# Cross attention: value and output weights multiplied per head, probabilities packed, and the load of projected values issued ahead of the store

## What is computed

```python
h1 = adaln(x, t, norm1_w, norm1_b)
x = mha(h1, h1, attn1_wq, attn1_wk, attn1_wv, attn1_wo, attn1_bo) + x
h2 = adaln(x, t, norm2_w, norm2_b)
x = mha(h2, context, attn2_wq, attn2_wk, attn2_wv, attn2_wo, attn2_bo) + x
...
    scores = jnp.einsum('bhqd,bhkd->bhqk', q, k) / math.sqrt(DH)
    attn = jax.nn.softmax(scores, axis=-1)
    out = jnp.einsum('bhqk,bhkd->bhqd', attn, v)
    out = out.transpose(0, 2, 1, 3).reshape(b, sq, INNER)
    return out @ wo + bo
```

## Time and profile before

| | before |
|---|---|
| median of 3 runs | 931.8 us (930.72 to 932.12) |
| the profiled execution | 932.87 us, span 931.1 us |
| mean granted clock of TensorE | 0.917 |
| busy: PE, PEld | 796.0 us (85%), 666.3 us (72%) |
| busy: DVE, ACT, POOL | 568.6 (61%), 540.7 (58%), 360.9 us (39%) |
| L685, transposes of probabilities | 512 records, 77.7 us |
| L697, probabilities by values | 1024 records, 70.2 us |
| L650 on oTB, output product | 256 records, 32.9 us |
| L641 on ctxT, value projection | 36 records in the trace, 18.6 us |

### The profile page before, as it was taken

How to read it: one execution, slowest core, us unless ns; L and a number is a source line. 1 busy time by engine, 2 the same in 40 slices (tenths; PEclk the granted TensorE clock), 3 DMA queues, 4 the chain that set the end, 5 groups by cost and what they waited for, 6 DMA issues and landing times.

```text
span 931.1 us, 19002 instructions
## 1 busy us (share of the span) xinstructions
PE 796.0 (85%) x6173; PEld 666.3 (72%) x6173; DVE 568.6 (61%) x1941; ACT 540.7 (58%) x1147; POOL 360.9 (39%) x559
## 2 busy tenths in 40 slices
PE   5989999999999999999987688999977776861693
PEld 4767778878788888888866456999746565651693
DVE  1687778777776767766674352333458787885012
ACT  3656677666776667666764222333448898851462
POOL 1344344333433323233655150566413222226362
PEclk9999999999999999999998689999956979795797
DMA  9532033206030001000200131888500000001574
GB/s 280 198 129 107 1 129 129 106 2 231 5 120 34 19 2 37 16 23 16 65 12 19 46 105 47 241 252 246 201 18 1 1 0 1 1 1 38 164 204 125
DMA packets 43612, 78.50 MB, mean 84 GB/s; under 512 B 5564, under 2 KB 28812, under 8 KB 42876
## 3 DMA queue, kind: packets, MB, share of 16 engines
q1 hardware_dynamic: 40027, 70.09, 23.5%
q0 software_dynamic: 3488, 7.20, 2.2%
HBM read 63.98 MB, written 30.13 MB: 101 GB/s over the span
## 4 chain that ended last, share of the span: by engine, by line
PE 56%; DVE 21%; issue 8%; ACT 6%; POOL 6%; DMA 2%; DVEq 0%; SPq 0%; ACTq 0%; POOLq 0%
PE bank L635 6%; PE bank L909 5%; PE bank L697 5%; PE bank L660 4%; PE bank L650 3%; DVE sb_smax L1406 3%; PE bank L641 3%; PE bank L685 3%; PE bank L669 3%; PE bank L917 3%; DVE sb_row_sum L1416 3%; PE bank L1018 2%; DVE sb_st_all L1714 2%; PE bank L726 2%; PE bank L1026 2%
## 5 line engine op out<-in xcount | busy, mean ns | idle before, releaser
L1891 POOL TENSOR_TENSOR sb_expd<-sb_expd,sb_rden 128x512 f32<-128x512 f32 (+1 forms) x128 | 112.5, 880 | 248.3 <-DVE sb_rden L1420 248.2
L1406 DVE TENSOR_REDUCE sb_smax<-bank 128x4 f32<-128x512 f32 (+1 forms) x128 | 74.1, 579 | 59.1 <-PE bank L660 34.8
L1983 POOL TENSOR_TENSOR sb_rstd_all<-sb_rsq_all,sb_halves 128x4 f32<-128x4 f32 x44 | 45.2, 1028 | 130.7 <-DVE sb_rsq_all L1721 130.7
L685 PE MATMUL bank<-sb_eye,sb_expd 128*128 128x128 f32 (+1 forms) x512 | 77.7, 279 | 5.8 <-POOL sb_expd L1891 5.3
L1128 ACT ACTIVATE sb_expd<-sb_shifted 128x512 f32<-128x512 f32 (+1 forms) x128 | 69.8, 545 | 19.0 <-DVE sb_shifted L1409 18.0
L685 PEld LDWEIGHTS bank<-sb_eye,sb_expd 128*128 128x128 f32 (+1 forms) x512 | 60.0, 145 | 26.4 <-issue 13.2
L1122 ACT ACTIVATE sb_probT<-bank 128x512 f32<-128x512 f32 (+1 forms) x128 | 74.3, 590 | 7.2 <-PE bank L685 7.0
L1409 DVE TENSOR_TENSOR sb_shifted<-bank,sb_smax 128x512 f32<-128x512 f32 (+1 forms) x128 | 75.0, 586 | 4.4
L1416 DVE TENSOR_REDUCE sb_row_sum<-sb_expd 128x4 f32<-128x512 f32 (+1 forms) x128 | 73.0, 570 | 5.5 <-ACT sb_expd L1128 5.5
L635 PE MATMUL bank<-sb_h1T,sb_watt 128*128 128x128 f32 x512 | 71.6, 286 | 4.7 <-ACT sb_h1T L1045 2.3
L697 PE MATMUL bank<-sb_probT,sb_v 128*64 128x128 f32 (+1 forms) x1024 | 70.2, 279 | 5.0 <-issue 3.4
(11 more groups left out here) (256 smaller groups left out, 1905.7 us busy)
## 6 DMA issues: line engine op xcount, KB each, us to landing
sb_up_w<-gate_up SPq DMA_DIRECT2D x38, 384.0 KB, 4.1
rows_b<-pad_b SPq DMA_DIRECT2D x7, 1105.0 KB, 8.5
rows_a<-pad_a SPq DMA_DIRECT2D x7, 975.0 KB, 6.4
sb_up_w<-w1b SPq DMA_DIRECT2D x23, 256.0 KB, 3.5
sb_v<-v_all SPq DMA_DIRECT2D x16, 308.0 KB
v_all<-sb_v_rows SPq DMA_DIRECT2D x9, 512.0 KB, 2.6
sb_blk_x<-rows_a SPq DMA_DIRECT2D x38, 65.0 KB, 3.0
sb_watt<-att_w SPq DMA_DIRECT2D x4, 512.0 KB, 6.6
```

What stands on the lines that cost most here:

```text
L685: mm = pe.transpose(trans[u % 2][0:n, h, :], expd[:, (units_before(i) + u) % EXP_RING, h, 0:n], eye[:, :])
L1406: dve.tensor_reduce(smax[:, u % 2, :], s_in, X, ALU.max).then_inc(max_done, 1)
L1891: pool.tensor_tensor(e, e, rden[:, u % 2, :].unsqueeze(2).broadcast_to([P, QH, n]), ALU.mult).then_inc(norm_done, 1)
```

## The change

Per head, `softmax(...) v wo` is computed as probabilities times (context times (wv wo)). In iteration 0 four new fills `b2_0` to `b2_3` multiply the value weights of each head by its output weights into `b2` (128 by 16 heads of 128), which takes the place of the value and output weights of block B. A projected row of context is then 16 heads of 128 instead of 16 of 64, so the value projection is four fills `v2_0` to `v2_3`, made and stored in two halves through the same `v2_rows`. The DRAM tensor `v2_all` holds for each block its 16 x 77 = 1232 rows of 128, heads one after another, and a block's rows are loaded in 10 chunks of 128 partitions (the last has 80).

The probabilities of block B are kept for all 16 heads side by side in `expd2` (1232 columns), transposed in 10 chunks of 128 columns across heads instead of 16 of 77, in groups of 2, 2, 3 and 3, and copied to `probT2`. The value products of block B, their copies by ScalarE and `oTB` are gone. `wo2` is ten accumulating products of `probT2` with the loaded values (`cross_out`). The ring `expd` is block A's alone. The Gelu is written in place, which frees `gact`.

`FILL` changes: the value projections stand in steps 6, 7, 9 and 10 (before: 0 and 4), `v1_1` moves from step 7 to the last one, `zT` from step 10 to the last one, ahead of `v1_1` and `logit`. SyncE issues `load_values(i - 1)` at the start of iteration i, ahead of `store_values(i)`; before it was `store_values(i)` and then `load_values(i)`. The load for a block now waits for the output product two blocks before, instead of its value products.

```diff
 FILL = [
-    (("h2T", "v2_0"), ("g2_5",)),
+    (("h2T",), ("g2_5",)),
     (("a2_0", "a2_1"), ("a2_2", "wo2", "rank")),
-    (("q1_1",), ("k1_0",)),
-    (("k1_1", "a2_3"), ("q1_0",)),
-    (("h3T", "v2_1"), ("g2_4",)),
-    (("g2_0", "g2_1", "g2_3"), ("gate",)),
-    (("lin",), ()),
-    (("v1_1",), ()),
+    (("q1_1", "b2_0"), ("k1_0",)),
+    (("k1_1", "a2_3"), ("q1_0", "b2_1")),
+    (("h3T", "b2_2"), ("g2_4",)),
+    (("g2_0", "g2_1", "g2_3"), ("gate", "b2_3")),
+    (("lin",), ("v2_0",)),
+    (("v2_1",), ()),
     (("wo1",), ("g2_2", "ffout")),
-    ((), ("hT",)),
-    ((), ("v1_0", "zT")),
-    (("logit",), ()),
+    (("v2_2",), ("hT",)),
+    ((), ("v1_0", "v2_3")),
+    (("zT", "v1_1"), ("logit",)),
 ]
...
             def store_values(i):
                 n = V2_BLOCK[i]
-                last = min(P, B * C - P * n)
-                sp.wait_ge(emptied["act"], max(PLAN[i, "v2_0"][2], PLAN[i, "v2_1"][2]))
-                sp.dma_start(v2_all[P * n:P * n + last, :], v2_rows[0:last, :]).then_inc(v2_stored, 16)
+                by_batch = v2_all.rearrange("(b h k) d -> b k h d", h=H, k=C)
+                for half in range(2):
+                    sp.wait_ge(emptied["act"], max(PLAN[i, f"v2_{2 * half + j}"][2] for j in range(2)))
+                    for b, k0, k1, p0, p1 in v2_pieces(n):
+                        sp.dma_start(by_batch[b, k0:k1, 8 * half:8 * half + 8, :],
+                                     v2_rows[p0:p1, :].rearrange("p (h d) -> p h d", h=8)).then_inc(v2_stored, 16)
...
             def load_values(b):
-                sp.wait_ge(v2_stored, 16 * v2_blocks(b))
+
+                sp.wait_ge(v2_stored, 16 * v2_stores(v2_blocks(b)))
                 if b >= 2:
-                    sp.wait_ge(pv_done, units_before(b) // 2)
...
+                    sp.wait_ge(proj_full, PLAN[b, "wo2"][1])
...
             def values(i):
+                if i >= 1:
+                    load_values(i - 1)
                 if i in V2_BLOCK:
                     store_values(i)
-                load_values(i)
...
+            def cross_out(i, name):
+
+                t = use(i, name)
+                for c in range(CHUNKS):
+                    k = min(P, H * C - P * c)
+                    mm = pe.matmul(t[:, 0:D], probT2[0:k, c, :], v2[0:k, i % 2, c, :], start=(c == 0), stop=(c == CHUNKS - 1))
                 mm.then_inc(proj_full, 1)
...
                 if name == "wo2":
-                    pe.wait_ge(o_kept, at(i, lambda t: units_before(t) // 2))
-                    if is_iteration(i, 2):
-                        pe.wait_ge(ld_wo2, 16)
-                    o_proj(i, name, "B", wo[1])
+                    pe.wait_ge(probT_ready, units_before(i))
+                    pe.wait_ge(v2_in[i % 2], 32 * (i // 2))
+                    cross_out(i, name)
...
                 if name[:2] == "v2":
                     n = V2_BLOCK[i]
                     last = min(P, B * C - P * n)
-                    if n and name == last_of(i, "v2", first=True):
-                        act.wait_ge(v2_stored, 16 * n)
-                    empty(i, name, v2_rows[0:last, half * 512:(half + 1) * 512], lambda t: t[0:last, :])
+                    if name == "v2_0":
+                        from_one(act, v2_stored, 16 * v2_stores(n))
+                    if name == "v2_2":
+                        act.wait_ge(v2_stored, 16 * (v2_stores(n) + len(v2_pieces(n))))
+                    empty(i, name, v2_rows[0:last, half % 2 * 512:(half % 2 + 1) * 512], lambda t: t[0:last, :])
```

More of the change, by code:

```diff
@@ L158, in present @@
 def present(i, name):
-    if name[:2] == "a2":
+    if name[:2] in ("a2", "b2"):
         return i == 0
@@ L180, with v2_pieces, v2_stores @@
 V2_BLOCK = {i: v2_blocks(i) - 1 for i in range(B) if v2_blocks(i) > v2_blocks(i - 1)}
+def v2_pieces(n):
+    found, last = [], min(P * (n + 1), B * C)
+    for b in range(P * n // C, -(-last // C)):
+        first, end = max(P * n, C * b), min(last, C * (b + 1))
+        found.append((b, first - C * b, end - C * b, first - P * n, end - P * n))
+    return found
+def v2_stores(n):
+    return 2 * sum(len(v2_pieces(m)) for m in range(n))
 def proj_plan():
@@ L201, in units_before, with pairs_before @@
     return sum(QH * (("A" in streams(j)) + ("B" in streams(j))) for j in range(-1, i))
+def pairs_before(i):
+    return sum(QH // 2 for j in range(-1, i) if "A" in streams(j))
 def units(S, steps):
@@ L536, in empty_rows @@
                     sp.dma_start(*(v[part, :].rearrange("(p n) d -> p (n d)", p=P) for v in (t, pad))).then_inc(zeroed, 16)
-            for i in range(B):
+            for i in range(B + 1):
                 values(i)
@@ L719, in fill @@
                         mm = pe.matmul(t[:, h * P:(h + 1) * P], qk2_w[p, 1, c, :], qk2_w[p, 0, c, :], start=True, stop=True)
+                    mm.then_inc(proj_full, 1)
+                if name.startswith("b2"):
+                    if name == "b2_0":
+                        pe.wait_ge(ld_vo2, 32)
+                    t, j = use(i, name), int(name[-1])
+                    p = slice(DH * (j % 2), DH * (j % 2) + DH)
+                    for h in range(QH):
+                        c = 4 * (j // 2) + h
+                        mm = pe.matmul(t[:, h * P:(h + 1) * P], vo2_w[p, 0, c, :], vo2_w[p, 1, c, :], start=True, stop=True)
                     mm.then_inc(proj_full, 1)
@@ L730, in fill @@
                     if i == 0:
-                        pe.wait_ge(ld_att2, 48)
+                        emptied_by(0, "b2_3")
                     rows_ = slice(P * V2_BLOCK[i], min(P * V2_BLOCK[i] + P, B * C))
-                    v_proj(i, name, wv[1], ctxT[:, rows_], half, rows_.stop - rows_.start)
+                    v_proj(i, name, b2, ctxT[:, rows_], int(name[-1]), rows_.stop - rows_.start)
                 if name.startswith("q1"):
```

140 lines of the change are left out of this document (80 added, 60 removed).

## The result

| | before | after |
|---|---|---|
| median of 4 runs | 931.6 us (930.72 to 932.12) | 977.75 us (976.19 to 978.34) |
| span of the profiled execution | 931.1 us | 976.5 us |
| mean granted clock of TensorE | 0.917 | 0.895 |

The ratio is 1.0494 (95% interval 1.0476 to 1.0512). The change makes the kernel 46 us slower, where 3.5 were forecast and 940 us was the end of the range.

The account below looks back on a forecast made before the run. TensorE's throughput was taken to bind most of an iteration, with a second chain close behind. The profiled 932.9 us plus 0.5 for the iterations and 3.0 for the clock, less 1.1, gave 935.3 us; range 926 to 940.

Parts of the forecast that it names:

- Late store: Rival, chance 0.12: ScalarE's copy of v2_2 waits for the first half's store; 937.5 to 945 us.
- The term's threshold: In Late store: the half's landing after v2_1's copy decides from about 3.8 us; at 5 us nine iterations lose about 0.9 each.
- The clock: Term: TensorE's granted clock falls to 0.50 in about two of iterations 5, 7, 10 and 12, +3 us, bounds 0 and +6.
- if the clock stays at 1.00 through 120 to 460: Sign of being wrong: TensorE's granted clock never falls between 120 and 460 us of the profile.
- Without projection: Iterations without a value projection: 10 and 12 gain 1.25 us each, 5 and 7 gain 0.5 each.
- Odd with projection: Iterations 3, 9, 11 and 13, with a value projection: -0.25 us each, -1.0 together.
- Even: Iterations 4, 6, 8 and 14, with a value projection: +0.1 us each, +0.4 together.
- Iteration 0: No block B work to remove; b2 fills, two more projections and v1_1 add +5.2 us, between 4.5 and 6.
- Iterations 15 to 17: Iteration 15 unchanged; in 16 and 17 the output product's wait for ScalarE's copy goes, -0.4 and -0.6 us.
- The sum without the late store: Likeliest case, chance 0.42: iterations +0.5 and two falls of the clock +3.0, 935.3 us, between 933.7 and 937.5.
- The chain behind TensorE: From block A's last value product through Gelu, exponentials, x and norm to zC's transpose; it limits gains in 5, 7, 10, 12.
- if v2_2's copy is released after +27.5: Sign of being wrong: ScalarE's store wait at the v2_2 copy, expected to end by +26.7 us, ends after +27.5.

Follow-up runs that it names:

- the kernel with pieces cut at 16: The changed kernel with each piece of the value store cut once more, into a multiple of 16 partitions and the rest: 1.0164 of before (946.9 us).
- both edits: The changed kernel with store pieces cut at multiples of 16 partitions and a second buffer for a projection's second half: 1.0018 of before, 1.0006 when run again.
- a variant: On top of both edits, either the load of projected values back in its old place (1.0068) or the b2 fills placed later (1.0059).
- the kernel with the cut stores: The kernel before, with its ten value stores cut in two, each at its own partition count (one after 127, one after 53): 0.999 of before.

## Why the prediction was wrong, point by point

**The failed step** is in the rival "Late store": "So the half should land 2.6 to 3.3 us after v2_1's copy". It took the landing from a 512 KB store and a 128 KB load, both of 128 partitions, and allowed issue time for the pieces. The waiting copies were released 3.3 to 12.3 us after the first issue, which follows v2_1's copy at once; with one store of 128 partitions it was 3.2, as the step has it. The longest can be estimated from the rate of one engine: 53 partitions and 5 of the other 75 are (53 + 5) x 8 packets of 512 B, 238 KB, at 22 GB/s 10.8 us. The store of 128 partitions, with 8 on each engine, leaves 1.7 of its 3.2 us for the rest, which makes 12.5. The term's threshold held: from about 4 us on it costs. Its price didn't: at 5 us an iteration was to lose about 0.9, and the kernel with pieces cut at 16 lost 2.0 there. Nor did its end: nothing in the profile bounded the landing at 5 us. With 10.49 us of idle ScalarE iteration 8 lost 9.7.

**What I weighed it against** was the Trainium skill's rule on two transfers to disjoint partition halves (DMA: Bandwidth & Descriptors, Rules for kernel authors), by which both go over the same 16 engines. The longest landing was not of that kind: the 53 partitions went at the rate of one engine. By that rule I had put three pieces at 6.6 us and some 945; the halves of three pieces took 4.5 to 8.6, and those of two up to 12.3. And that a 128 KB load and a 512 KB store land together I read as "most of a landing looks like fixed delay". Both were 128 partitions wide; where the width changed, the landing did.

**The clock.** Forecast: it falls in two of iterations 5, 7, 10 and 12, for +3. It began to fall in none, in either kernel. With both edits those four idle 2.0 to 3.2 us each, and two stretches at the end of iteration 10 read 1.00:

```profile
346.40:349.80 3.40, 1.97 (x9) 0.91 (x10) 1.96 (x10) 1.60 (x4) 2.10 (x5) 1.00 0.01 2
347.60:351.00 3.40, 2.44 (x10) 1.13 (x9) 1.16 (x6) 1.60 (x4) 1.95 (x5) 1.00 0.01 2
```

I had worked out 1.5 us of TensorE work in 3.4 behind ffout; in the emptier of these two it was 2.0, and in the next, with v1_1 (1.02) behind zC, 2.4. On the list of signs of being wrong was "if the clock stays at 1.00 through 120 to 460", and with both edits it did. In the changed kernel it fell instead behind the store's waits (in iterations 0, 1, 3, 8, 11 and 13). With both edits it fell in iteration 1, which took 2.3 us more against +0.4; one stretch of 3.4 us at half speed explains at most 1.7 of that. So the 3 us of this term were right in no place.

**The iterations**, taken from the kernel with both edits, where no late store covers them. Without projection: -0.8 and -0.7 (5, 7) against -0.5, -1.4 and -1.1 (10, 12) against -1.25: right. Odd with projection: -0.7, -0.4, -0.3, -0.6 against -0.25: right in kind. Even: -0.1, -0.4, 0.0, -0.3 against +0.1. The second pair starts 4.0 to 4.2 us after the first, where 4.0 to 4.1 was forecast. Iteration 0: +6.3 against +5.2 (the parts that the prediction names, 3.7 - 0.86 - 0.69 + 3.3, are 5.45), of it 3.7 for the fills, as forecast; the other projections cost 2.6 instead of 1.5. In the changed kernel it was +12.1, with the store's 4.46 us and a fallen clock. Iterations 0 to 14 sum to +2.1 us, and by their own terms to +1.5. In the second trace of the same kernel they sum to +6.3, with b2_0's wait and a fallen clock in iterations 0 and 1. Iterations 15 to 17, from pair 0 to the last router product, were to lose 1.0 and took 67.1 us before and after, and 69.4 with both edits. The output products of 16 and 17 no longer wait, as forecast, but the clock is at 0.50 when they run: 4.31 and 4.61 us for 20 records in the first trace with both edits, 3.55 and 2.05 for 16 before.

**The sum without the late store** was 935.3 us, 1.004 of before. The kernels without it gave 1.0006 to 1.0068. That they lie so near is partly luck: 3 of the 3.5 us were for a fall of the clock that didn't come where it was put, and in its place iterations 0 and 1 cost 3 us more than forecast and those with a projection 2.3 less. The chain behind TensorE in iterations 5, 7, 10 and 12 was read rightly, and the forecast missed its range by one transfer. What would have shown it stood in the prediction's own list: "if v2_2's copy is released after +27.5"; in iteration 8 it was released at +35.2.

**What stays open.** In one place the kernels with both edits and a variant came out at 1.006 to 1.007, in the others at 1.001 to 1.003. From iteration 3 to 14 the traces of those with unmoved projections agree. Behind the last router product 404 to 408 us follow instead of 401 in the kernel with the cut stores, which is otherwise the kernel before, at the same place. The work there is the same, and the mean granted clock is 0.83 instead of 0.84, which over 404 us can be a few us. I ran nothing that tells why the clock differs. That b2_0's wait for its weights explains the spread between runs of one kernel is argued, not shown.

## What to carry to other kernels

Before a store is cut along partitions, factor the counts: here a piece went only as wide as its largest divisor up to 16, and 53 or 127 partitions were one engine at 22 to 27 GB/s. The pieces of one store behaved as if they shared an engine, so add up what each puts on it. Cutting it further buys width with issue time of 0.6 us a DMA; a second buffer, which takes the transfer off the path, was worth more and needed no new memory, only space that was free at that time. When a landing time is taken from another transfer, take it from one of the same width, and price a wait on it at what it would be if it came four times as late.
